# Reordering the projections, copies and routing of a sixteen-batch patch-attention and expert kernel, and splitting the last batch's scores into pairs of banks

## The reference

```
h   = patches of 8, 16 and 32 frames (half-overlapping), each projected to 128, plus bias, position, scale
      -> 127 + 63 + 31 = 221 tokens per batch, 16 batches
h   = h + attention(layernorm(h))      8 heads of 16, softmax over the batch's 221 tokens, output projection, bias
out = h + experts(layernorm(h))        1024 tokens, top-2 of 8 experts, gelu(x @ w1[e]) @ w2[e], weighted sum
```

## Time and profile before

| what | value |
|---|---|
| runs of the kernel | 306.54, 309.08, 309.54 us; median 309.08 us |
| the profiled execution | 307.14 us, of which the span is 305.3 us |
| TensorE busy | 269.8 us, 88% of the span |
| VectorE busy | 199.5 us, 65% |
| ScalarE busy | 143.3 us, 47% |
| GpSimd busy | 109.4 us, 36% |
| mean granted TensorE clock | 0.935 |

### The profile page before, as it was taken

How to read it: one execution, slowest core, us unless ns; L and a number is a source line. 1 busy time by engine, 2 the same in 40 slices (tenths; PEclk the granted TensorE clock), 3 DMA queues, 4 the chain that set the end, 5 groups by cost and what they waited for, 6 DMA issues and landing times.

```text
span 305.3 us, 7681 instructions
## 1 busy us (share of the span) xinstructions
PE 269.8 (88%) x3147; PEld 230.8 (76%) x3147; DVE 199.5 (65%) x440; ACT 143.3 (47%) x220; POOL 109.4 (36%) x172
## 2 busy tenths in 40 slices
PE   8999869889999999999979798998979797998461
PEld 8999859677879797979768696877868696877331
DVE  4786674787888678785745567574756656475654
ACT  4650414533434352525456557564666466565220
POOL 4000220102455555555614264543636272422200
PEclk9999988999999999999979889997999899899755
DMA  7999000394000000000210020111011010001241
GB/s 206 380 381 422 9 1 2 84 344 125 20 10 24 15 22 15 18 24 13 68 29 17 11 54 17 36 34 37 26 34 37 10 52 11 17 26 35 78 136 46
DMA packets 19466, 22.33 MB, mean 73 GB/s; under 512 B 2416, under 2 KB 15448, under 8 KB 19400
## 3 DMA queue, kind: packets, MB, share of 16 engines
q1 hardware_dynamic: 17671, 19.24, 20.1%
q0 software_dynamic: 1760, 2.60, 2.8%
HBM read 17.42 MB, written 5.95 MB: 77 GB/s over the span
## 4 chain that ended last, share of the span: by engine, by line
PE 69%; DVE 12%; issue 6%; ACT 6%; DMA 4%; POOL 1%; SPq 0%; DVEq 0%; POOLq 0%; ACTq 0%
PE e_ps L982 13%; PE s_ps L1065 12%; PE s_ps L982 7%; PE e_ps L1186 7%; DVE nmax L801 7%; PE m_ps L1050 5%; PE m_ps L1173 4%; PE m_ps L1131 4%; PE s_ps L1118 3%; PE e_ps L1173 2%; PE m_ps L1040 2%; PE m_ps L1142 2%; DMA x_raw<-x 2%; DMA y_rows<-y_sb,idx_u 2%; ACT hidT L588 1%
## 5 line engine op out<-in xcount | busy, mean ns | idle before, releaser
L801 DVE TENSOR_REDUCE nmax<-s_ps 128x4 fp32r<-128x884 f32 (+1 forms) x64 | 65.9, 1071 | 24.8 <-PE s_ps L1065 24.8
L573 ACT ACTIVATE probs<-s_ps 128x888 f32<-128x888 f32 (+1 forms) x64 | 54.7, 906 | 57.9 <-PE s_ps L1118 57.9
L473 POOL DMA_INDIRECT y_rows<-y_sb,idx_u x23 | 23.0, 999 | 62.5 <-PE s_ps L1118 40.2
L1131 PE MATMUL m_ps<-probs,v_aug 93*32 93x221 f32 (+1 forms) x512 | 28.8, 366 | 0.7 <-ACT probs L573 0.7
L454 POOL DMA_INDIRECT z_slots<-z,slot_u x20 | 22.6, 1128 | 16.4 <-PE s_ps L1118 11.8
L1050 PE MATMUL m_ps<-zT,wqkv_sb 128*128 128x221 f32 x64 | 17.3, 397 | 11.4 <-ACT h_sb L553 11.4
L426 POOL TENSOR_TENSOR var_eps<-mv,eps_t 128x2 f32<-128x2 f32 x16 | 3.2, 201 | 66.4 <-DVE mv L768 66.2
L1186 PE MATMUL e_ps<-w_now,hidT 128*128 128x128 f32 x184 | 25.3, 290 | 0.0
L786 DVE TENSOR_TENSOR k_lo<-m_ps,k_hi 128x442 fp32r<-128x442 f32 x16 | 9.9, 619 | 23.6 <-ACT k_hi L566 23.6
L1186 PEld LDWEIGHTS e_ps<-w_now,hidT 128*128 128x128 f32 x184 | 23.2, 203 | 1.3 <-issue 1.0
L1065 PE MATMUL s_ps<-k_hi,q_a 32*128 32x222 f32 (+1 forms) x256 | 18.5, 308 | 4.6 <-DVE nmax L801 3.3
(11 more groups left out here) (125 smaller groups left out, 619.6 us busy)
## 6 DMA issues: line engine op xcount, KB each, us to landing
w_raw<-wt SPq DMA_DIRECT2D x6, 512.0 KB, 9.5
x_raw<-x SPq DMA_DIRECT2D x6, 512.0 KB, 9.9
w_sb<-w SPq DMA_DIRECT2D x1, 2048.0 KB, 9.6
z_slots<-z SPq DMA_DIRECT2D x1, 1518.0 KB, 9.5
zs<-z_slots SPq DMA_DIRECT2D x7, 198.0 KB, 2.6
x_raw<-x SPq DMA_DIRECT2D x4, 256.0 KB, 5.1
out<-h SPq DMA_DIRECT2D x11, 64.0 KB
c_sb<-consts SPq DMA_DIRECT2D x1, 599.0 KB, 11.6
```

The source lines that it names most:

```text
L473: g.indirect_dma_start(y_dram, bass.IndirectOffsetOnAxis(ap=idx_u[:, at:at + 1], axis=0), y_sb[:, i, :], None).then_inc(y_out, 16)
L573: s.activation(probs[0:n, blk, 2 * f:2 * f + 2].rearrange("p t u n -> p t (u n)"), s_ps[0:n, 2 * f:2 * f + 2, 0:2 * NE], ACT.Exp, scale=DH ...
L801: v.tensor_reduce(nmax[0:n, blk, 2 * f:2 * f + 2, 0:2], src, AX_X, ALU.max, negate=True).then_inc(max_ready, 1)
L1131: mm = pe.matmul(bank[32 * t:32 * t + 32, :], v_aug[0:n, b % 2, blk, HALF * r + t, :], probs[0:n, blk, t, r, 0:N], start=(blk == 0), stop= ...
```

## The change

It does the following.

1. In every cycle `project_k(c+1)` is issued behind the second scores of block 0 and no longer behind `place_max`. In cycles with experts ScalarE's `h_copy` is ahead of `q_high`.
2. VectorE's `y_evac` and the `hT_evac` of a unit that ended in the cycle before go ahead of `maxima(c,0)`; `zsT_evac` goes ahead of `norm`; `y_sb` has two buffers.
3. The plan of the filler: four steps in front of `s1(c,1)` in cycles 1 to 6, taken from those behind the second scores of block 0; cycle 0 has other numbers as well.
4. `route_slots` goes from the end of VectorE's cycle 0 to a place ahead of `k_low`; `v_copy(0)` and `lo_x(7)` go behind `maxima(0,0)`, and `project_q(1)` gets a wait for that copy.
5. GpSimd's `hb` waits for `z_ready` in place of `h_ready`.
6. `zs_turn(0)` goes ahead of `pv(6)` in cycle 7; later `zs_turn` wait for two tiles' gelus of the round before and not for all.
7. Cycle 15 has an order of its own (`last_cycle`): scores, maxima, placement, second scores and exponentials go by pairs of banks, the first half of the turned maxima is copied by ScalarE, and `aggregate(14)` is followed by three matmuls on zeros. In cycle 16 eight matmuls on zeros stand between `pv(15)` and `aggregate(15)`.
8. At the end three of the four parts of `combine` go ahead of `turn(15)`.

The diff, cut (waits and counters of the new buffers and semaphores, and the split of `combine` and `pv` into parts, are left out where the list says them):

```diff
-PLAN = {..., -1: (4, 8, 0, 2, 6), 0: (18, 10, 0, 14, 6), 1: (0, 10, 0, 18, 20), ... 6: (0, 10, 0, 18, 20)}
-KEEP = {}
+PLAN = {..., -1: (4, 8, 0, 2, 6), 0: (18, 8, 0, 10, 12), 1: (4, 10, 0, 14, 20), ... 6: (4, 10, 0, 14, 20)}
+KEEP = {BATCH - 1: 3, BATCH: 8}
@@ GpSimd, stage1
-                pool.wait_ge(h_ready, b + 1)
+                pool.wait_ge(z_ready, b * 2 + 2)
@@ ScalarE
+            def half_nmaxT_copy(b):
+                act.wait_ge(max_placed, b + 1)
+                s.copy(nmaxT[0:64], m_ps[0:64, 2, 0:NE]).then_inc(max_half, 1)
...
+                if experts and c + 2 < BATCH:
+                    h_copy(c + 2)
                 if 0 <= c + 1 < BATCH:
                     q_high(c + 1)
-                if c + 2 < BATCH:
+                if not experts and c + 2 < BATCH:
                     h_copy(c + 2)
...
+                if c == BATCH - 1:
+                    half_nmaxT_copy(c)
@@ VectorE, the cycle
                 n = c - E0
+                if (c - 1, 1) in UNIT_ENDS:
+                    hT_evac(UNIT_ENDS[(c - 1, 1)])
+                y_evac(n - 1)
                 if 0 <= c < BATCH:
                     maxima(c, 0)
-                if (c - 1, 1) in UNIT_ENDS:
-                    hT_evac(UNIT_ENDS[(c - 1, 1)])
+                if c == 0:
+                    v_copy(0)
+                    lo_x(7)
...
-                y_evac(n - 1)
                 if 0 <= c < BATCH:
                     maxima(c, 1)
                 if c == BATCH:
-                    combine(0)
+                    combine(0, 0)
+                    combine(0, 1)
+                    combine(1, 0)
+                if c == BATCH - 1:
+                    nmaxT_copy(c)
                 if c - 1 >= 0:
                     turn(c - 1)
...
+                if n >= 0:
+                    zsT_evac(n + 1)
                 if c - 1 >= 0:
                     norm(c - 1)
-                if n >= 0:
-                    zsT_evac(n + 1)
...
                     ln_stats(c + 2)
+                if c == 0:
+                    route_slots()
                 if 0 <= c + 1 < BATCH:
                     k_low(c + 1)
...
-                if c == 0:
-                    lo_x(7)
-                    route_slots()
...
                 if c == BATCH:
-                    combine(1)
+                    combine(1, 1)
@@ TensorE
+            def place_pair(b, f):
+                pe.wait_ge(max_ready, 4 * b + 3 + f)
+                ...
+                for blk in range(2):
+                    n = TILE_N[blk]
+                    w = P if blk == 0 else NE - P
+                    mm = pe.matmul(m_ps[64 * f:64 * f + 64, 2, P * blk:P * blk + w],
+                                   nmax[0:n, blk, 2 * f:2 * f + 2].rearrange("p t r -> p (t r)").bitcast(F32),
+                                   ident[0:n, 0:w], start=True, stop=True)
+                mm.then_inc(max_placed, 1)
...
+            def last_cycle(b):
+                s1_pair(b, 0, 0)
+                s1_pair(b, 0, 1)
+                pv(b - 1, range(0, 1))
+                s1_pair(b, 1, 0)
+                pv(b - 1, range(1, 2))
+                s1_pair(b, 1, 1)
+                place_pair(b, 0)
+                s2_pair_products(b, 0, 0)
+                place_pair(b, 1)
+                s2_pair_maxima(b, 0, 0)
+                s2_pair_products(b, 0, 1)
+                s2_pair_maxima(b, 0, 1)
+                for f in range(2):
+                    s2_pair_products(b, 1, f)
+                    s2_pair_maxima(b, 1, f)
+                aggregate(b - 1)
...
             for c in range(-2, BATCH + 1):
+                if c == BATCH - 1:
+                    last_cycle(c)
+                    keep(KEEP[c], y_ready, ROUNDS)
+                    continue
+                if c == BATCH:
+                    pv(c - 1)
+                    keep(KEEP[c], y_ready, ROUNDS)
+                    aggregate(c - 1)
+                    continue
...
+                if n == 0:
+                    zs_turn(0)
                 if behind:
                     pv(c - 1)
-                if n == 0:
-                    zs_turn(0)
...
                     place_max(c)
-                if ahead1:
-                    project_k(c + 1)
                 if n >= 0:
                     zs_turn(n + 1)
                 tok_some(pm)
                 if here:
                     s2_products(c, 0)
                     s2_maxima(c, 0)
+                if ahead1:
+                    project_k(c + 1)
                 tok_some(p3)
```

More of the change, by code:

```diff
@@ L366, in load_y @@
             def load_y():
-                sp.wait_ge(y_out, 16 * N_TILES)
+                for i in range(2):
+                    sp.wait_ge(y_out[i], 16 * sum(ROUND_TILES[i::2]))
                 y = y_dram[0:T_FFN * TOP_K].rearrange("(n k) d -> n (k d)", k=TOP_K)
@@ L850, in ffn_z, with combine @@
                                     ALU.subtract, ALU.mult).then_inc(z2_ready, 1)
[L852 removed]
+            def combine(t, k):
                 dve.wait_ge(ew_in, 16)
                 dve.wait_ge(y_in[t], 16 * (len(SPANS[t]) + 1))
[L855 to L858, removed]
[L859 to L862 removed]
+                for b in range(FFN_B):
+                    n, j = ffn_rows(b, t), table(b, t)
+                    if k:
+                        dve.wait_ge(combined, t * FFN_B * TOP_K + b + 1)
+                    v.scalar_tensor_tensor(out=h1k[0:n, b, t, :], in0=g_sb[0:n, j, k, :],
+                                           scalar=ew_sb[0:n, j, k:k + 1], in1=h1k[0:n, b, t, :],
+                                           op0=ALU.mult, op1=ALU.add).then_inc(combined, 1)
             def zsT_evac(n):
@@ L1058, in project_v, with four @@
                           stop=True).then_inc(v_done, 1)
-            def four(dst, a, b, blk, u, start, stop):
+            def four(dst, a, b, blk, u, start, stop, heads=range(HALF)):
                 n = TILE_N[blk]
-                for t in range(HALF):
+                for t in heads:
                     rs = slice(32 * t, 32 * t + 32)
@@ L1084, in s1, with s1_pair @@
                 mm.then_inc(s1_done, 1)
+            def s1_pair(b, blk, f):
+                if blk:
+                    pe.wait_ge(max_ready, 4 * b + 1 + f)
+                elif f == 0:
+                    pe.wait_ge(q_ready, b + 1)
+                    pe.wait_ge(k_ready, b + 1)
+                    pe.wait_ge(probs_ready, 4 * b)
+                heads = range(2 * f, 2 * f + 2)
+                q, kh, kl = q_a[:, b % 2], k_hi[:, b % 2], k_lo[:, b % 2]
+                for u in range(2):
+                    four(s_ps, q, kh, blk, u, True, False, heads)
+                    mm = four(s_ps, q, kl, blk, u, False, True, heads)
+                mm.then_inc(s1_done, 1)
@@ new lines, in s2_pair_products @@
+            def s2_pair_products(b, blk, f):
+                if blk:
+                    pe.wait_ge(probs_ready, 4 * b + 1 + f)
+                else:
+                    pe.wait_ge(max_ready, 4 * b + 3 + f)
+                heads = range(2 * f, 2 * f + 2)
+                q, kh, kl = q_a[:, b % 2], k_hi[:, b % 2], k_lo[:, b % 2]
+                for u in range(2):
+                    four(s_ps, kh, q, blk, u, u == 0, False, heads)
+                    four(s_ps, kl, q, blk, u, False, False, heads)
@@ new lines, in s2_pair_maxima @@
+            def s2_pair_maxima(b, blk, f):
+                n = TILE_N[blk]
+                if f:
+                    pe.wait_ge(nmaxT_ready, b + 1)
+                else:
+                    pe.wait_ge(max_half, 1)
+                for u in range(2):
+                    for t in range(2 * f, 2 * f + 2):
+                        rs = slice(32 * t, 32 * t + 32)
+                        mm = pe.matmul(s_ps[0:n, t, u * NE:(u + 1) * NE], sel_r[rs, u, 0:n], nmaxT[rs, :],
+                                       start=False, stop=(u == 1))
+                mm.then_inc(s2_done, 1)
@@ L1120, in s2_maxima, with pv @@
                 mm.then_inc(s2_done, 1)
-            def pv(b):
+            def pv(b, rs=range(2)):
                 pe.wait_ge(probs_ready, b * 4 + 4)
                 pe.wait_ge(v_ready, min(b + 2, BATCH))
-                for r in range(2):
+                for r in rs:
                     bank = m_ps[:, 0, r * N:(r + 1) * N]
@@ L1265, in _ @@
                 tok_some(p4)
-                keep(k4, *free)
 def constants(np):
```

59 lines of the change are left out of this document (33 added, 26 removed).

## The result

| | before | after |
|---|---|---|
| runs | 306.54 to 309.54 us, median 309.06 (4 runs) | 276.27 to 278.20 us, median 277.14 (4 runs) |
| profiled execution, span | 307.14, 305.3 us | 276.9, 275.1 us |
| mean granted TensorE clock | 0.935 | 0.993 |

The ratio of the two is 0.898, 95% interval 0.893 to 0.904: 32 us, or 10%, faster. The forecast was 281 with a range of 278 to 288, so the direction and most of the size were right, and the time lies under the range. By the profiled executions the sum was 281.2 against 276.9.

The account below looks back on a forecast made before the run. TensorE was taken as full in cycles 2 to 6, elsewhere losing time to waits, chiefly project_k for h_copy, and clock falls; the tail to latency. 307.14 - 16.3 - 0 - 3.8 - 1.65 - 0.5 + 0.1 - 3.8 = 281.2, so 281; range 278 to 288.

Parts of the forecast that it names:

- cycles 8 to 13: Expert cycles: project_k's wait for h_copy goes and the clock holds, 14.42 us each, 86.5 in place of 102.82: -16.3 us.
- cycle 7: The 1.6 us wait goes, but zs_turn(0) ahead of pv(6) costs 1.65: sum 0, between -1.6 and +1.
- cycle 0: Early hT_evac shortens the filler's wait and avoids a clock fall; lo_x(7) delays place_max by 0.75: -3.8, between -2.5 and -4.5.
- cycle 1: route_slots leaves the end of cycle 0, where it holds up maxima(1,0) and TensorE for 1.77 us: -1.65.
- cycles 2 to 6: Four filler steps fill the 0.20 us maxima wait, less 0.15 a cycle for nmaxT_copy: -0.5 us.
- cycle 14: Same case as cycles 2 to 6, the maxima's matmuls now waiting for nmaxT_copy: +0.1 us.
- tail: From cycle 15's start: pairs of banks and early combine parts shorten 25.13 us to 21.3: -3.8, between -2.6 and -4.6.
- the walk: Step-by-step timing of the tail: exponentials done at 9.0, combine's rows earlier, turn and norm until 15.5, end at 21.0 us.
- go back and forth: Rival: short, frequent idling makes the clock fall in four of cycles 8 to 13, 1.56 us each: 287 us; chance 0.12.
- the 2.66 of the Trainium skill: ScalarE's table switch, weighed and not used: h about 1.2 us later per cycle, sum some 7 us less good.
- The tail's rival: The tail gives nothing, since TensorE at its lower clock does the extra matmuls in the chain: 285 us; chance 0.10.
- GpSimd's later wait for z: Some 1 to 1.5 us per cycle, forecast to cost nothing; rival: GpSimd falls behind, 312 us, chance 0.03.

Follow-up runs that it names:

- both put back: The changed kernel with project_k behind place_max and h_copy behind q_high, both as before: 302.37 us, ratio 0.980 to the kernel before.
- late evacuations: The changed kernel with hT_evac and y_evac behind maxima(c,0) again: 288.28 us, ratio 0.948 to the kernel before.
- h back: The changed kernel with h_copy behind q_high again, project_k staying behind the second scores: 283.69 us, ratio 0.919 to the kernel before.
- k back: The changed kernel with project_k back behind place_max, h_copy staying ahead of q_high: 291.0 us, ratio 0.941 to the kernel before.
- k and h alone: The kernel before with only project_k behind the second scores of block 0 and h_copy ahead of q_high: 289.14 us, ratio 0.935.
- route back: The changed kernel with route_slots, lo_x(7) and v_copy(0) where they were in VectorE's list: 279.18 us, ratio 0.911 to the kernel before.

## Why the prediction was wrong, step by step

The sum against the trace, as changes to the profiled execution:

| step | forecast | measured |
|---|---|---|
| cycles 8 to 13 | -16.3 | -17.7 |
| cycle 7 | 0 | -2.1 |
| cycle 0 | -3.8 | -4.1 |
| cycle 1 | -1.65 | -1.6 |
| cycles 2 to 6 | -0.5 | -0.7 |
| cycle 14 | +0.1 | +0.05 |
| tail | -3.8 | -4.2 |

The rest, 0.1 us, is the start of cycle 0. **No row went the wrong way and two sizes were off; the tail's size came right with a wrong cause for its end.**

*The step that failed is "Cycle 7 ... Sum: 0".* It took the clock to fall behind the wait for the expert rows, and named -1.6 as the bound if it holds. In the profiled execution it held (1.00, 16.83 us), which is worth the 1.5 us of a fall; the wait for `h_copy` that went was 1.80 and not 1.6, and the move of `zs_turn`, taken at 1.65, cost 1.5 to 1.6 by the traces with it put back. In part this is chance: of the ten traces with this wait at its full length, in eight programs, the clock fell behind it in seven, but of the changed kernel's own three in one. Of the other three executions of the result only the mean clock is on record, 0.986 to 0.992. With a fall in cycle 7 the median of 277.14 would be near 278.6 and inside the range (an estimate from the 1.5 us of a fall).

*The second is "each cycle is 16.06 - 1.64 = 14.42".* The wait was read from the idle column, and took 1.80 by start to start, and 0.1 more came from `down`, whose sixteen matmuls take 1.95 in place of 2.05. With both put back, cycle 8 was 1.89 longer. Six times 0.24 is the 1.4 us.

*The smaller rows.* In cycle 0 `place_max` was held up by 0.36 us and not 0.75. In cycles 2 to 6 the 0.15 us a cycle set down for `nmaxT_copy` did not appear: TensorE is busy for all of their 71.06 us. The eight matmuls on zeros took 2.05 us and not the 3.2 read from the warm-up.

*The tail.* Exponentials done at 9.8 us and not 9.0, `aggregate(15)` at 15.6 against 15.5, end at 20.96 against the 21.0 of the walk; the 0.3 added for the lower clock was not needed in this trace and is needed in others. That it came so near is in part luck. The walk let `combine` start at 9.65 us because its rows would land then. It started at 9.85, but the rows were there before; it stood behind the residual of batch 14, which the walk left out. In the changed kernel `aggregate(14)` and `combine` set the end. The load sets it only where it is issued late, as in the kernel before and in the run with the late evacuations. Whether `combine` ahead of that residual is faster was not tested.

*The range.* The bounds on the fast side that the text itself names (cycle 7 -1.6, cycle 0 -0.7, the tail -0.8, cycles 2 to 6 -0.7) come to 277.4 together, and the range stopped at 278. Cycle 7 went past its bound (-2.1); the other three gained only 0.2 to 0.4 each over the forecast. The expert cycles, the largest term, gained 1.4 more than forecast and had been given no bound at all.

The rivals. The clock did not go back and forth in cycles 8 to 13 of the changed kernel, and waits of 1.1 us, one in each cycle, left it at 1.00; waits of 1.6 us, as often, let it fall 10 times in 14. The Trainium skill's rule on short, frequent idling (TensorE: Matmul & The Clock Gate, A second HAM failure mode: psum-queue depth-cycling) agrees with this case at the longer waits alone. The table load took 1.28 us and `h_copy` began 0.12 behind its end (178.15 and 178.27), so the 2.66 of the Trainium skill (ScalarE: Activation LUTs, What ACT_TABLE_LOAD costs) does not hold in this queue. The distance from h to k, 0.05 to 0.1 us, held in each of the seven cycles: the cycles repeat closely, 14.15 to 14.20 us for 8 to 13. The tail's rival, that TensorE at its lower clock takes the gain away, came true in one execution of the changed kernel (24.81 us). GpSimd's later wait for z cost nothing that the trace shows: it waited 12.8 us in all, and no wait of TensorE for it follows.

## What to carry to other kernels

A stall has three prices: its length from start to start (the idle column is short by the modelled end of the last matmul), a fall of the clock behind it if it is long (from 1.6 us on in these runs, and then not each time), and the spread that falls bring into the runs. Sum the latencies of both parties of a wait before moving either: moving k alone or h alone left 0.48 or 1.33 us a cycle, moving both left none, and moving either one was enough to end the clock's falls in these cycles. Where a change reorders several lists, look for pairs that only work together, like the early evacuation and the filler steps in front of which it stands. And read what the last chain really waits for: a forecast can meet the time by a wrong cause.

## What the runs showed of the hardware

How often the granted clock fell behind one wait of TensorE, over all 17 traces, ahead of the tail, for waits of over 1 us and the 0.4 us of h back, by the wait's length in the idle column:

| wait | traces or cycles | fell |
|---|---|---|
| `project_k` for `h_copy`, 0.4 us (h back) | 7 | 0 |
| the same, 1.1 us (k back) | 7 | 0 |
| the same, 1.6 us (before, and both back) | 14 | 10 |
| late exponentials in cycle 6, 1.6 to 1.8 us | 7 | 3 |
| the expert rows, 1.8 to 2.2 us | 10 | 7 |
| `hT_evac` in cycle 0, 2.5 us (before, k and h alone, late evacuations) | 3 | 3 |
| the maxima in cycle 1, 1.2 to 1.8 us (before, k and h alone, route back) | 3 | 0 |
| the high parts of x at the start, 1.3 to 2.1 us | 5 | 0 |

A fall costs about 1.5 us each time. Between 1.6 and 2.2 us of idle time the same wait of the same kernel fell in one execution or cycle and held in another; what decides it is not settled by these runs. The last two rows, where none fell, say that the length is not all.

ScalarE's exponentials of batch 6, block 0, began about 2.4 us late in all seven traces from two of the chips, at the same instruction in seven different programs, and in none of the eight from two others. TensorE lost 1.6 to 1.8 us by it. The profile names no releaser, and no run tested a cause.
